# A decoder block on one core: transposed probabilities may also be written to the two filler banks, by a table made at build time

## What is computed

```python
x = x + attn(layernorm(x))                        # causal, q/k/v/o weights and biases
x = x + xattn(layernorm(x), ctx, ctx)             # causal, heads of ctx as keys and values, no weights
x = x + ffn(layernorm(x))                         # relu(x Wup^T) Wdown^T + sum(softmax(top2)) * (x Wexpert)
```

## Time and profile before

| | us |
|---|---|
| time of the profiled execution | 767.26 |
| its span (first to last instruction) | 765.4 |
| median of the runs | 767.93 |
| TensorE busy (matmul) | 696.5 |
| TensorE weight load | 530.6 |
| ACT busy | 514.4 |
| DVE busy | 505.9 |
| POOL busy | 256.3 |
| mean granted clock | 0.975 of 2.4 GHz |

### The profile page before, as it was taken

The page is one execution under the profiler, slowest core; times in us unless marked ns, Lnnn a source line. Parts: engine busy times, 40 slices in busy tenths (PEclk is TensorE's granted clock), DMA queues, the critical chain, the costliest instruction groups (busy, mean ns, idle before and its releaser), DMA issues.

```text
span 765.4 us, 14496 instructions
## 1 busy us (share of the span) xinstructions
PE 696.5 (91%) x4480; PEld 530.6 (69%) x4480; DVE 505.9 (66%) x1726; ACT 514.4 (67%) x1450; POOL 256.3 (33%) x390
## 2 busy tenths in 40 slices
PE   4998999989998998988768977899988999899998
PEld 3875787767777776765545745677766777677786
DVE  5567676666767766666757677767886667764622
ACT  6578877667777777677868676876777776773110
POOL 2645544323554346523542365311221101001000
PEclk9999999999999999999989987999989999999999
DMA  9553433346332553438544594434353443510101
GB/s 317 143 146 84 120 68 75 85 117 186 76 78 65 171 152 83 102 78 260 127 106 104 147 282 100 110 91 110 84 156 93 111 97 76 152 36 1 56 1 55
DMA packets 52331, 86.16 MB, mean 113 GB/s; under 512 B 8608, under 2 KB 16800, under 8 KB 52256
## 3 DMA queue, kind: packets, MB, share of 16 engines
q1 hardware_dynamic: 52256, 85.25, 42.5%
HBM read 27.55 MB, written 7.34 MB: 46 GB/s over the span
## 4 chain that ended last, share of the span: by engine, by line
PE 77%; ACT 7%; DVE 6%; issue 5%; POOL 2%; DMA 1%; SPq 1%; DVEq 0%; POOLq 0%
PE t L433 16%; PE m L472 14%; PE m L473 13%; PE m L474 13%; PE pv L466 10%; PE s L418 8%; ACT probs L838 3%; DVE probs L618 3%; ACT prob L847 2%; POOL probs L945 1%; PE m L487 1%; PE pv L487 1%; DMA prob<-in_kT 1%; DVE prob L628 1%; PE pv L573 1%
## 5 line engine op out<-in xcount | busy, mean ns | idle before, releaser
L838 ACT ACTIVATE probs<-probs,negmax 128x128 f32<-128x128 f32 (+3 forms) x512 | 285.7, 558 | 106.9 <-DVE negmax L618 99.3
L618 DVE CUSTOM_DVE_ANT_0 probs<-s,mask 128x128 f32<-128x128 f32 (+3 forms) x512 | 249.1, 488 | 153.5 <-PE s L418 151.5
L433 PE MATMUL t<-ident,probs 128*128 128x128 f32 x1280 | 234.6, 283 | 44.8 <-ACT prob L847 32.5
L433 PEld LDWEIGHTS t<-ident,probs 128*128 128x128 f32 x1280 | 161.2, 143 | 111.6 <-ACT prob L847 51.7
L418 PE MATMUL s<-stack 96*128 96x128 f32 (+3 forms) x512 | 204.2, 401 | 0.0
L945 POOL TENSOR_SCALAR probs<-probs,rsum 128x128 f32<-128x128 f32 (+3 forms) x256 | 132.7, 537 | 206.8 <-DVE rsum L632 202.5
L847 ACT ACTIVATE prob<-t 128x512 f32<-128x512 f32 (+1 forms) x256 | 136.1, 532 | 69.5 <-PE t L433 69.4
L628 DVE COPY prob<-t 128x256 f32<-128x256 f32 (+1 forms) x256 | 91.2, 356 | 22.9 <-PE t L433 22.4
L418 PEld LDWEIGHTS s<-stack 96*128 96x128 f32 x512 | 100.4, 196 | 8.4 <-DMA stack<-stage 0.3
L838 ACT ACTIVATION_READ_ACCUMULATOR probs<-probs,negmax 128x1 f32 x512 | 96.5, 189 | 0.0
L472 PE MATMUL m<-xT_hi,w_lo 128*128 128x512 f32 x192 | 79.8, 416 | 0.9 <-DVE xT_lo L684 0.9
(11 more groups left out here) (132 smaller groups left out, 915.8 us busy)
## 6 DMA issues: line engine op xcount, KB each, us to landing
stack<-stage SPq DMA_DIRECT2D x384, 128.0 KB, 2.3
xt<-in_x SPq DMA_DIRECT2D x16, 256.0 KB, 4.1
xres<-in_x SPq DMA_DIRECT2D x4, 1024.0 KB, 5.8
kraw<-in_ctxT SPq DMA_DIRECT2D x16, 256.0 KB, 2.9
cv<-in_ctx SPq DMA_DIRECT2D x16, 256.0 KB, 3.1
x<-xres SPq DMA_DIRECT2D x3, 1024.0 KB, 4.6
res<-x SPq DMA_DIRECT2D x8, 256.0 KB, 6.1
out<-res SPq DMA_DIRECT2D x2, 1024.0 KB, 4.5
```

The costliest lines, as they stand in the source:

```text
L433: mm = nc.tensor.transpose(dst[:, chunk(qb - kb)], probs[:, (2 * P + h) % 3, OFF[qb] + PART * kb:OFF[qb] + PART * kb + PART], ident[:, :])
L618: nc.vector.tensor_tensor_reduce(probs[:, (2 * P + h) % 3, OFF[qb]:OFF[qb + 1]], score_tile(P, i), mask[:, T - N:T], -SCALE, BIG, ALU.add, ...
L838: nc.scalar.activation(tile, tile, ACT.Exp, bias=negmax[:, P % 2, h, qb:qb + 1], scale=-1.0, accum_out=total).then_inc(p_exp, 1)
```

## The change

`plan` also makes a table of which bank each turn writes. For each of the 512 turns it lists the two t banks and, from z = 9 on, each m bank whose last filler ended at least two slots earlier and whose next one begins at least four slots later, and takes the one whose last use began longest ago. TURN_BEFORE holds who had the bank before: another turn (key "T"), or a filler. BEFORE of a filler is made anew, since a turn may now have been there last. `turn` waits for whatever stood in its bank, by `emptied`, which knows the new kind; the copies read from the bank of the table through `turned_tile`. Order, number and size of all instructions on all engines stay as they were; only banks and what some waits are on differ.

```diff
--- before.py
+++ after.py
@@ -173,10 +173,39 @@
         bank_of[key] = 2
         running.setdefault(z, []).append((key, 0))
         ended.setdefault(z + 1, []).append(key)
-    return bank_of, before, running, ended
-
-
-BANK_OF, BEFORE, RUNNING, ENDED = plan()
+    spans = [sorted((z, z + slots + held, key) for z, slots, held, key in jobs if bank_of[key] == n) for n in range(2)]
+    users = {n: [(z, end, key) for z, end, key in spans[n]] for n in range(2)}
+    latest = {("t", n): None for n in range(NTB)}
+    stamp = {("t", n): -10 ** 6 + n for n in range(NTB)}
+    turn_bank, turn_before = {}, {}
+    for P in range(NP):
+        for i in range(PAIRS):
+            z = PAIRS * P + i
+            choice = [("t", n) for n in range(NTB)]
+            for n in range(2):
+                if z > PAIRS and all(end + 2 <= z or start >= z + 4 for start, end, key in users[n] if key[0] != "T"):
+                    choice.append(("m", n))
+            at = {c: max([start for start, end, key in users[c[1]] if start < z], default=-10 ** 6) if c[0] == "m" else stamp[c]
+                  for c in choice}
+            best = min(choice, key=lambda c: at[c])
+            turn_bank[P, i] = best
+            if best[0] == "t":
+                turn_before[P, i] = latest[best]
+                latest[best], stamp[best] = ("T", P, i), z
+            else:
+                users[best[1]].append((z, z + 1, ("T", P, i)))
+    for n in range(2):
+        prior = None
+        for start, end, key in sorted(users[n]):
+            if key[0] == "T":
+                turn_before[key[1:]] = prior
+            else:
+                before[key] = prior
+            prior = key
+    return bank_of, before, running, ended, turn_bank, turn_before
+
+
+BANK_OF, BEFORE, RUNNING, ENDED, TURN_BANK, TURN_BEFORE = plan()
 
 
 def decoder_block(nc, dram):
@@ -296,6 +325,8 @@
         def emptied(key):
 
             kind, n, m = key if len(key) == 3 else (*key, 0)
+            if kind == "T":
+                return copied(n, m)
             return {"L": (lnt_lo, KC * n + m + 1), "Q": (q_lo, SELF_AT[n] + 1 if kind == "Q" else 0), "K": (k_lo, n + 1), "V": (v_out, NT * n + m + 1),
                     "O": (o_out, NT * n + m + 1), "FL": (fl_lo, KC * n + m + 1),
                     "FG": (gate_out, n + 1), "FU": (h_lo_done, KC * n + m + 1), "FE": (exp_out, NT * n + m + 1),
@@ -305,7 +336,8 @@
             return s_bank[(PAIRS * P + i) % NS][:, 0:PART * (i % NT + 1)]
 
         def turned_tile(P, i):
-            return t_bank[(PAIRS * P + i) % NTB][:, 0:T - PART * (i % NT)]
+            kind, n = TURN_BANK[P, i]
+            return (t_bank if kind == "t" else m_bank)[n][:, 0:T - PART * (i % NT)]
 
         def out_bank(key):
             return [*m_bank, pv_bank][BANK_OF[key]]
@@ -426,8 +458,8 @@
                         pe.wait_ge(p_done, PAIRS * own_rank(P) + NT * (h + 1))
                     else:
                         pe.wait_ge(p_exp, PAIRS * P + NT * (h + 1))
-                if PAIRS * P + i >= NTB:
-                    pe.wait_ge(*(copied(P, i - NTB) if i >= NTB else copied(P - 1, PAIRS + i - NTB)))
+                if TURN_BEFORE[P, i] is not None:
+                    pe.wait_ge(*emptied(TURN_BEFORE[P, i]))
                 dst = turned_tile(P, i)
                 for qb in range(kb, NT):
                     mm = nc.tensor.transpose(dst[:, chunk(qb - kb)],
```

## The result

The kernel after took 757.3 us, the median of 4 runs (754.35 to 761.06), beside 768.07 for the kernel before (4 runs, 767.79 to 769.16): on record as 0.9881 of its time, with a 95% interval of 0.9845 to 0.9918. (The quotient of the two medians is 0.9860. The profiled execution took 758.24 us against 767.26, its span 756.3 against 765.4, its mean clock 0.981 against 0.975: 9.1 us less span, where the working had 11.1.

The account below looks back on a forecast made before the run. In steps without fillers no engine is full: they take turns, TensorE waiting mostly for ACT's and DVE's bank copies. Terms 9.5 + 1.6 (clock) = 11.1 us off 767.26 gave 756.2, plus 0.67 to the median: 756.9; range 752 to 763.5.

Parts of the forecast that it names:

- Ends of pairs: Steps 29, 36, 39: filler or values start once ACT's copy of slot 4 lands; 1.2, 1.1 and 1.4 us.
- the part of step 36 up to its filler: Step 36: filler follows ACT's copy of slot 4, out at 416.66, instead of starting at 417.82; 1.1 us.
- Steps 2 to 4: Steps 2 to 4: 0.5 us, estimated after step 31, since a Q bank and an L bank are used.
- Steps 32 and 33: Steps 32, 33: DVE's two score waits go, the middle moves up 1.0, DVE's slot 7 copy is last; 2.0 us.
- Steps 40 and 41, 51: Steps 40, 41: DVE's copy bounds the values, 0.5 us; step 51: FL needs the last normalised row, 0.3 us.
- The clock: Drops to 1.2 GHz after stalls thin out: 1.6 us from pairs 29, 33, 39, 51, bounds 0 and 4.
- Step 42 gave nothing: Step 42: no gain; DVE stands 3.57 us behind POOL's weight split, TensorE's wait moves to the scores.
- The lists: TensorE's turn waits on copies fall from 38 to under 12 us; new waits total some 15 us.
- Turn (30, 6): Step 30, slot 6: a wait longer than before would show the prediction wrong.
- Rival 1: Whole kernel: the stalls return in full, 32 us, time 736; chance 0.04.
- Rival 2: Waits only renamed; only ends of steps 29, 36, 39 give something: 0 to 4 us, 764 to 768; chance 0.17.
- Rival 3: Slower by the clock: drops fall where TensorE is the bound (steps 26, 37, 38, 43 on), 1 us each; chance 0.03.

Follow-up runs that it names:

- same, repeats: Kernel before, banks unchanged, with the three transposes of slot 5 done three times in ten steps: 761.18 us, 0.9947 [0.9922, 0.9972].
- The three kernels with repeats: Transposes repeated in the kernel before, 761.18 us; in the kernel after, 754.62 us; in the kernel after with POOL's weight splits ahead of the layer-norm scale, 752.18 us.

## Why the prediction came out

**Ends of pairs: right, but for one wait.** From the end of one values block to the next, in the three traces whose difference is only banks or only clock (us; worked out from the TensorE timelines; for step 33 in the kernel before, for example, 388.55 + 3.27 less 370.54 + 2.36, the end of the values block after step 31, makes 18.92, or 18.93 before rounding):

```
after step         27     29     31     33     35     37     39     41     51     59
before          22.47  18.55  18.03  18.93  19.69  19.00  19.25  18.74  20.35  20.15
same, repeats   22.42  17.36  18.02  16.97  19.68  19.00  18.04  19.05  19.05  20.15
after           21.88  16.01  17.41  16.09  19.19  18.14  16.83  19.98  21.29  19.88
```

From the second line to the third is the banks' part: 0.54, 1.35, 0.61, 0.88, 0.49, 0.86 and 1.21 for the pairs to step 39, and 0.27 for the last. Forecast: 0.8, 1.2, 0.5, 2.0, 0.8, 1.1, 1.4 and 0.4. The four pairs after 29, 33, 37 and 39 ran at full clock in both traces, 4.3 us together. In the pair after 35 the kernel after had 6.8 us at 1.2 GHz against 3.4, so its 0.49 is rather too low. From the kernel before to the kernel after, the part of step 36 up to its filler gave 1.1, its forecast, and the filled step 37 lost 0.2. Steps 2 to 4 gave 0.24 (0.5 forecast), and the pair after 41, for which the forecast had nothing, 0.35. The forecast named ACT's copy of slot 4 as the next wait in steps 29, 36 and 39. The rows show that wait in 29 and 39, 0.05 and 0.14 us behind the copy, the latter just outside the 0.1 that was given. In step 36 the number came out and the wait did not: TensorE stood at scores, behind DVE's maximum, and it is luck that this ended with the copy.

**Steps 32 and 33: the term that was mis-sized.** "DVE's two waits for them, 0.58 and 0.44 us, go [...]; then DVE, ACT's copy [...] and the rest move up 1.0." They do go, but the bank isn't needed for it: the repeats take them away with two banks, by the clock. On top of that the bank's part is 0.9 us, not 2.0. Clock and bank together took 2.84 us off this pair (18.93 to 16.09). That DVE's copy of slot 7 would be last was right: it ended at 384.61, the values at 384.66 + 0.43 = 385.09, 0.48 later and not 0.25 (0.4 was given as the most), as the last part starts anew behind it.

**Steps 40 and 41, 51.** TensorE's start of the values moved by 0.38 us in the first (0.5 forecast) and by 0.54 at 51 (0.3 forecast; FL waits 0.58 us for the normalised row, as the forecast had it). Both were lost again, since the values behind them ran at 1.2 GHz.

**The clock: right in sign, misjudged in kind.** Forecast 1.6 us as a little under half of four pairs' drops. In the profile the drops of 29, 33 and 39 went, worth 17.36, 16.97 and 18.04 against 18.55, 18.93 and 19.25 = 4.4 us; that of 51 stayed and grew (20.35 - 19.05 = 1.3 us before; after, 21.29 against 18.88 with repeats = 2.4), and the pair with 41 got one more, 19.98 against 18.74 - 0.38 = 18.36, 1.6. Steps 42 and 43 took 22.85 before and 22.54 with repeats, which I count with the clock, though both traces have one stretch of 6.8 us at 1.2 GHz there; the kernel after has 3.4 us and 22.19. So the 0.66 us of these two steps aren't told apart between clock and banks. Net 4.4 + 0.3 - 1.1 - 1.6 = 2.0, or 1.9 before rounding. The number was near, but it is a balance of 4.7 won and 2.7 moved, and it differs from one execution to the next. The Trainium skill, "TensorE: Matmul & The Clock Gate", section "A second HAM failure mode: psum-queue depth-cycling", has short idles between groups of matmuls as enough to make the clock go up and down. The traces agree: in step 33 of the kernel before drops came with stalls of 1.01 and 1.27 us, and work put into those stalls took them away.

**Sum.** Banks: 0.54 + 1.35 + 0.61 + 0.88 + 0.49 + 0.86 + 1.21 + 0.38 + 0.27, with 0.24 in steps 2 to 4, 0.35 in the pair after 41 (22.54 with repeats, 22.19 after) and 0.17 at 51 (19.05 less 18.88), less 0.07 in the pair to step 25 and 0.19 in that after 51: 7.1 us. With the clock's 1.9 it makes 9.0 of the 9.1 us of the spans. Forecast 9.5 + 1.6. The bank terms were 2.4 us too high: 1.1 of it is steps 32 and 33, 1.6 lies in eight other terms of 0.1 to 0.3 each, and two terms and the pair after 41 gave 0.6 more than forecast, less 0.3 lost in pairs that had no term. The clock's term was 0.3 too low.

**Step 42 gave nothing: right**, and the stall's new place too: 1.76 us at the scores. That a second piece (1.92) would stand at `back` wasn't foreseen.

**The lists.** Under 12 us of turn waits were forecast, 9.2 measured, 7.6 of them in steps 43, 52 and 60; some 15 of new ones, 17.5 measured (9.2 + 4.2 + 2.8 + 1.3), without the 3.2 behind DVE's stores. Turn (23, 6) has no wait and (31, 6) stands 1.18 us for 1.27. Turn (30, 6) stands 0.91 us for 0.84, for DVE's low half of Q instead of ACT's copy: a sign of being wrong that the prediction had named, and worth 0.07 us. Steps 5 to 23 and 44 to 49 kept their lengths to 0.04 us.

**The rivals.** Rival 1 (stalls back in full, 736) fell with step 42 and the ends of pairs. Rival 2 is right about the waits: TensorE's idle time fell by 2.5 us where 28.9 us had been taken away at turns, and one of the three ends of steps that it granted, step 36, has its wait at scores behind DVE, as it said. It fell on size. Rival 3's mechanism exists: 2.7 us in this profile, 1.58 and 1.26 us in two steps of another; as a way to end slower it was far too small. The Trainium skill, in the section "HAM oscillation — how this bites in real kernels" of "TensorE: Matmul & The Clock Gate", reports no gain from double-buffered PSUM in another kernel; here another bank gave 1.2%. And the Trainium skill's "Perfetto Trace Analysis", section "Matmul Optimizations", asks to use all 8 banks: lending idle ones to other work gave 1.2% by one table and cost 1.5% by a looser one.

## What to carry to other kernels

Where an engine waits for a bank, ask what it does next and whether that needs the same copy: only the work in between moves, and the wait in front of it is what the change is worth. Don't take the total of a wait for its worth: 13 us of turn waits more or less made no difference between two of these kernels. Give a shared bank to work only when its last user's slowest reader is done with room to spare; the table with two slots of distance gained 1.2%, the one with one slot (and half the distance ahead of the next filler) cost 1.5%. And before a stall is priced, look whether TensorE was at 1.2 GHz around it: a wait of another engine for its results may be the clock's, which a few redundant transposes can show in one run.

## What the runs showed of the hardware that was not expected

- Redundant work made an unchanged schedule faster: three times the transposes of slot 5 in ten steps took 0.53% off (0.9947 [0.9922, 0.9972]), as 20.4 us of 1.2 GHz went.
- The places of the drops vary without any edit ahead of them: one at 73 us makes step 4 13.18 us long in both profiles of the kernel after, and it is absent, at 11.55 or 11.56 us, in those of four kernels whose step 4 is the same. Yet the two profiles of one kernel agree in five of six places. The kernel before ran between 761 and 772 us over the later comparisons, where four runs had first shown 767.79 to 769.16. The three kernels with repeats scattered less: 1.3 us in 4 runs, 2.8 in 12 and 3.1 in 6, against 6.7 and 4.5 of the kernel after in 4 and 6 and 3.4 to 7.7 of the eight other variants in 5 to 12. Why a drop falls where it does stays open.
- A transfer put behind another on the same queue lost more than its place: the 1 MB weight landed 10.9 us after its issue behind 1 MB of residual rows and beside what was issued next, 5.8 us ahead of them, while the rows won 2.6 us (6.9 to 4.3). The loads of the stacked heads in the same stretch took 7.2 us in place of 5.7, and TensorE stood 2.55 us for one of them.
